# Attention scores in 32x32 tiles of TensorE, masks on three strips, masked blocks written once

## The reference, cut to what matters

```python
g = x @ Wg.T + bg;  v = x @ Wv.T + bv               # split in 16 heads of 8
corr = dot(g_i, g_j) / (|g_i| |g_j| + 1e-8)
m = (j <= i) & (j >= i - 128)                        # causal window of 128
corr = (corr * m + 1) / 2
denom = mean_j(corr) + 0.5
fitness_i = 1 / (denom_i * sum_i(1 / denom_i))
attn = softmax_j(corr_ij * fitness_i * m + (1 - m) * -1e10)
out = attn @ v
```

## Time and profile before

| | |
|---|---|
| median of 3 runs | 391.77 us (390.9 to 393.08) |
| profiled execution, its time | 388.9 us |
| its span, first to last instruction | 387.2 us |
| mean granted clock of TensorE | 0.933 |
| PE / DVE / ACT / POOL busy | 85% / 74% / 58% / 49% |
| matmuls | 2964 |

### The profile page before, as it was taken

The page is one execution under the profiler, slowest core; times in us unless marked ns, Lnnn a source line. Parts: engine busy times, 40 slices in busy tenths (PEclk is TensorE's granted clock), DMA queues, the critical chain, the costliest instruction groups (busy, mean ns, idle before and its releaser), DMA issues.

```text
span 387.2 us, 8903 instructions
## 1 busy us (share of the span) xinstructions
PE 329.0 (85%) x2964; PEld 195.8 (51%) x2964; DVE 285.7 (74%) x820; ACT 224.0 (58%) x498; POOL 188.0 (49%) x466
## 2 busy tenths in 40 slices
PE   6368786998899999999999999999998999857551
PEld 4233352554465656565656565656564656535341
DVE  1525547567879797979797979797979798889451
ACT  2034663466576767676767676767675777422210
POOL 7754033507273737373737474747473343543331
PEclk9999997799999999999999999999999999985555
DMA  4001000001000101010101010101010010000000
GB/s 117 27 1 29 14 2 3 27 2 29 1 30 3 42 1 42 2 44 1 42 2 43 1 43 2 43 0 30 3 29 13 15 30 2 14 14 3 14 14 17
DMA packets 12404, 7.62 MB, mean 20 GB/s; under 512 B 1026, under 2 KB 12356, under 8 KB 12356
## 3 DMA queue, kind: packets, MB, share of 16 engines
q1 hardware_dynamic: 12356, 7.03, 6.4%
HBM read 4.93 MB, written 2.10 MB: 18 GB/s over the span
## 4 chain that ended last, share of the span: by engine, by line
PE 34%; DVE 25%; POOL 18%; issue 13%; ACT 8%; POOLq 0%; ACTq 0%; DVEq 0%
PE OT L717 6%; PE S L694 5%; PE WA L824 4%; POOL nt L449 4%; PE S L698 3%; ACT Pm L545 3%; POOL rn L456 3%; POOL nt L451 3%; PE WC L737 2%; PE WD L795 2%; POOL nt L454 2%; POOL rstd L482 2%; DVE h L1065 2%; DVE xn L1113 2%; DVE A L1212 2%
## 5 line engine op out<-in xcount | busy, mean ns | idle before, releaser
L545 ACT ACTIVATE Pm<-S 128x384 f32<-128x384 f32 x256 | 111.8, 491 | 64.8 <-PE S L698 64.8
L694 PE MATMUL S<-mask,ident 128*128 128x384 f16 x256 | 65.8, 340 | 10.1 <-ACT Pm L545 7.9
L473 POOL TENSOR_TENSOR hq<-hm,hs 128x352 f32<-128x352 f32 x32 | 25.2, 787 | 66.0 <-DVE hm L1083 65.7
L717 PE MATMUL OT<-Pm,gv 128*32 128x256 f32 (+1 forms) x1024 | 56.8, 341 | 0.0
L698 PE MATMUL S<-BT,AT 32*128 32x256 f16 (+1 forms) x512 | 44.1, 251 | 0.0
L717 PEld LDWEIGHTS OT<-Pm,gv 128*32 128x32 f32 x1024 | 27.2, 111 | 21.2 <-issue 5.5
L698 PEld LDWEIGHTS S<-BT,AT 32*128 32x128 f16 x512 | 14.4, 93 | 42.9 <-issue 42.9
L694 PEld LDWEIGHTS S<-mask,ident 128*128 128x128 f16 x256 | 19.0, 99 | 33.7 <-issue 14.8
L1059 DVE SCALAR_TENSOR_TENSOR hh<-th,WC 128x352 f32<-128x352 f32 x32 | 16.6, 519 | 23.4 <-ACT th L563 23.3
L737 PE MATMUL WC<-wguT,xaT 128*128 128x352 f32 x64 | 29.1, 538 | 4.2 <-DVE h L1065 2.3
L795 PE MATMUL WD<-wdT,hqT 128*128 128x128 f32 (+1 forms) x192 | 29.6, 311 | 1.7 <-ACT hqT L593 1.7
(11 more groups left out here) (146 smaller groups left out, 715.0 us busy)
## 6 DMA issues: line engine op xcount, KB each, us to landing
xT<-x_turned_dram SPq DMA_DIRECT2D x16, 128.0 KB, 2.4
x_res<-x_dram SPq DMA_DIRECT2D x16, 128.0 KB, 2.1
out_dram<-yo SPq DMA_DIRECT2D x16, 128.0 KB, 2.1
wf<-w_down_dram SPq DMA_DIRECT2D x1, 176.0 KB, 2.5
wgv<-wgv_dram SPq DMA_DIRECT2D x1, 128.0 KB
wf<-w_gate_dram SPq DMA_DIRECT2D x1, 128.0 KB, 2.3
wf<-w_up_dram SPq DMA_DIRECT2D x1, 128.0 KB, 2.2
woT<-wo_dram SPq DMA_DIRECT2D x1, 64.0 KB
```

Of the source, the lines that this page charges most:

```text
L473: pool.tensor_tensor(b3(hq[:, k, 0:I]), b3(hm[:, k]), bc(hs[:, k], QB), ALU.mult).then_inc(s_hq, 1)
L545: act.activation(Pm[:, group % PR, hd % 4, :], S[:, (H * x + hd) % 3, 0:SCW], ACT.Exp, scale=1.0 / ZS).then_inc(s_exp, 1)
L694: pe.matmul(S[:, bank, 0:SCW], ident16[:, :], mask16[:, :], start=True, stop=False)
L717: i = pe.matmul(OT[VP * g:VP * (g + 1), T - (q1 - q0):T], gv_flat[:, at:at + VP], Pm[:, (GROUPS * x + c) % PR, g, q0:q1], start=(kt == 0 a ...
```

## The change

Three things change in `scores`, on PE:
- The dots come first, cut in groups of `KG = 32` keys. Each is a matmul on one 32x32 tile of the array (32 rows of the head, 32 keys): four tiles for keys 0 to 127 with the 160 queries that their window can reach, and four for keys 128 to 255 with 128, 96, 64 and 32 queries. So a pair has 16 of them.
- The mask comes last and only where a 32x32 block is partly masked: the diagonal blocks and the window's far edge, three strips of 32 columns in one matmul of 96 columns, one for each group of keys, eight for a pair. It uses the head's own row tile.
- Blocks that are wholly masked get no matmul. DVE writes them once, with nine memsets at the start (`s_far`), and nothing overwrites them. ACT waits for these before its first exp.

The semaphore `s_sc` is raised by the last mask matmul of a head. ACT's exp still reads all 384 columns.

```diff
+KG = 32
...
+        s_far = sem("s_far")
...
                 exps(t, 6)
                 if t == -1:
+                    act.wait_ge(s_far, 3 * (P // KG - 1))
                     exps(0, 0)
...
                 pair = [(2 * p + k, (H * x + 2 * p + k) % 3) for k in range(2)]
-                for hd, bank in pair:
-                    pe.matmul(S[:, bank, 0:SCW], ident16[:, :], mask16[:, :], start=True, stop=False)
-                for kt, (q0, q1) in enumerate(((0, T), (T, SCW))):
+                for kt in range(NT):
                     for hd, bank in pair:
                         r, c = 32 * (hd % 4), hd // 4
-                        i = pe.matmul(S[:, bank, q0:q1], AT[r:r + 32, x % 2, c, kt * P:(kt + 1) * P],
-                                      BT[r:r + 32, x % 2, c, T - (q1 - q0):T], start=False, stop=(kt == 1))
-                        if kt == 1:
-                            i.then_inc(s_sc, 1)
+                        for k0 in range(0, P, KG):
+                            at, n = (k0, P + KG) if kt == 0 else (T + k0, P - k0)
+                            q = kt * P + k0
+                            pe.matmul(S[k0:k0 + KG, bank, at:at + n], AT[r:r + 32, x % 2, c, q:q + KG],
+                                      BT[r:r + 32, x % 2, c, q:q + n], start=(kt == 0), stop=False)
+                near = mask16[:, :].rearrange("p (b c) -> p b c", c=P)
+                for n, (hd, bank) in enumerate(pair):
+                    m = 32 * (hd % 4)
+                    for k0 in range(0, P, KG):
+                        i = pe.matmul(S[k0:k0 + KG, bank, 0:SCW].rearrange("p (b c) -> p b c", c=P)[:, :, k0:k0 + KG],
+                                      ident16[m:m + KG, m:m + KG], near[m:m + KG, :, m:m + KG],
+                                      start=False, stop=True)
+                    i.then_inc(s_sc, 1)
...
         def _(dve):
+            for k0 in range(0, P, KG):
+                for a, b in ((0, k0), (k0 + P + KG, T), (T, T + k0)):
+                    if a < b:
+                        dve.memset(S[k0:k0 + KG, :, a:b], MASKED).then_inc(s_far, 1)
             dve.wait_ge(ld_b, 16 * 3)
```

## The result

The changed kernel takes 403.73 us (median of 4 runs, 401.97 to 404.55) against 392.38 for the kernel before on the same chip (390.9 to 393.08): ratio 1.0322, interval 1.0272 to 1.0372. It is slower by 11.4 us. The profiled execution took 401.97 us, its span is 400.3; before, 388.9 and 387.2.

A forecast was written before the change was run, and what follows sets the result against it. PE had almost no slack, but a chain through PE, ACT, DVE and POOL closed each turn. Terms: -4.0 - 1.6 - 2.5 + 11 - 0.15 + 2.0 = +4.75, 393.6 profiled, 396 median; range 390 to 402, overall 380 to 404.

The forecast's parts named there:

- A pair: PE's time for one pair of scores: 0.70 us before, 0.34 forecast, bounds 0.26 and 1.18.
- Rivals 2, 3 and 4: Pair costs 0.5 us: 386, chance 0.12; starts 25 ns apart: 392 to 393, 0.14; 49 ns: near 462, 0.05.
- The memsets: Nine DVE memsets of S at the start: some 3 us, all under the load of woT, cost 0.
- The clock in the loop: Main loop: PE's clock falls at the L818 wait, +1.1 us in 9 of 10 turns, +11; the eleventh -0.15.
- the chain's delay: PE work on the chain after L818, at low clock: between 0 and 3 us later, taken as 1.5.
- the saving in pair 6: The one pair of scores on the loop's chain gets shorter by 0.36 us a turn.
- The late stretch: 296 to 330 us, 16 pairs: PE could give 4.9 us, DVE's free time limits the gain to -2.5.
- the end: After 330 us, hanging on DVE and a slow PE: gain 0, an earlier clock fall +0.5 us.
- Falls in the first 62 us, where PE waits before many pairs, +1.5: Early part: clock falls at PE's waits before many pairs cost 1.5 us.
- the gains of 4.0 and 1.6: Shorter pairs on the chain: 12 in 24 to 62 us give -4.0, 5 in 67 to 84 us -1.6.
- Rival 1: The clock holds in spite of PE's waits: 379.2 us profiled, 382 as median; chance 0.27.
- The second circle: Loop through A, DVE's list, hh, seed, POOL, gh: 19.06 us a turn even with an infinitely fast scores step.

The follow-up runs named there:

- The experiment without masks: The kernel before with its mask matmuls left out, so its scores are unmasked: 400.88 us, ratio 1.0252.
- the two that give PE its work back: The changed kernel with fifteen unread matmuls ahead of PE's wait for xm: 390.08 us; the changed kernel with the old full-width masks issued as well: 390.88 us.
- the fills: Unread matmuls added to the changed kernel at the xm wait and in sequences 0 and 1: 385.6 us; with sixteen more before the weights' wait: 385.5 us.
- the kernel with wide dots: The changed kernel with strip masks kept but dots back in 32x128 tiles, far blocks unmasked: 404.7 us, ratio 1.0351.
- the profile with six fills: The changed kernel with six unread matmuls ahead of PE's wait for xm: nine executions at 390.5 to 394.1 us, two at 403.3 to 404.0, the profiled one among these.
- With the wait filled: The changed kernel with fifteen unread 256-column matmuls ahead of PE's wait for xm: 390.08 us, ratio 1.0008.
- the ramp filled: The changed kernel with four unread 256-column matmuls ahead of each pair's wait for ACT, sequences 0 and 1 only: 397.79 us, ratio 1.0244.
- both fills: The changed kernel with fifteen unread matmuls at PE's wait for xm and four ahead of each pair's wait in sequences 0 and 1: 385.6 us, ratio 0.9895.
- three: The kernel with both fills plus sixteen unread matmuls ahead of PE's wait for the gate and up weights: 385.5 us, ratio 0.9856.

## Why the prediction was right in direction and short in size

I had forecast +4.75 us; the profile has +13.1. As a median I had said 396, with 390 to 402 for this case; it is 403.73.

- **A pair.** Forecast 0.34 us, bounds 0.26 to 1.18; measured 0.28. Right, and a little too dear. Starts 3 to 4 ns apart held for eight matmuls on eight tiles; all 24 start within 0.149 us, which is 6.5 ns each, as reckoned. The Trainium skill's floor of about 25 ns ("TensorE: Matmul & The Clock Gate", "Wait — 56ns, not 53.3ns?") doesn't hold between different tiles; the 4 ns of the same page ("The mechanism") agree with the trace. Rivals 2, 3 and 4 fall with it.
- **The memsets.** Forecast some 3 us under the load of woT. DVE's first product starts at 4.67 us as before, and the memsets end at 3.15:

```profile
0.94 2.21 DVE L983 MEMSET S<- 32x288 f32 x9 [0.94 <-PEq L1521]
```

They took 2.21 us, all covered. Right.
- **The clock in the loop.** Forecast: a wait of 1.9 us at L818, the clock lost there in each turn, +1.1 a turn, +10.85 for the stretch. Measured 2.5 us, lost in each turn, 20.37 against 19.21, which is +1.16 in the turn shown, and +11.1 for the stretch. Right, in mechanism and size. Of its parts, the chain's delay was put at 1.5 and is 1.44 + 0.18 = 1.62 us; the saving in pair 6 was put at 0.36 and is 0.35. The experiment without masks and the two that give PE its work back show the cause. With the clock held a turn would be 18.8, so the low clock costs about 1.5 us a turn, of which the shorter pairs pay 0.4.
- **The late stretch.** Forecast -2.5, measured -1.8; the end, forecast +0.5, measured 0. Small misses.
- **The failed step** is "Falls in the first 62 us, where PE waits before many pairs, +1.5", beside the gains of 4.0 and 1.6: a net gain of 4.1 forecast up to 84 us, a loss of 3.9 measured. These 8.0 us are nearly the whole error of 8.3. The mechanism was named there and its size badly judged. Up to the fifth seed (63.85 us instead of 61.67) 2.2 us are lost where a net gain of 2.5 was forecast. Behind it another 1.7 are lost where 1.6 was to be gained: for that stretch the sum had no clock term at all, and the granted clock was 0.50 instead of 0.87 in 70 to 80. Up to 41 us the gain came, if less than reckoned: values start at 40.75 instead of 41.65, 0.9 against the 1.65 of five pairs at 0.33. Then the shorter pair leaves PE too little to do before ACT's exps are ready. The stretches of the changed kernel around it:

```profile
42.00:44.00 2.00, 0.69 (x27) 0.50 (x28) 0.64 (x2) 2.00 (x6) 0.00 (x0) 0.99 0.00 0
44.00:46.00 2.00, 1.94 (x41) 0.86 (x40) 1.86 (x6) 0.37 (x1) 0.96 (x4) 0.50 0.05 12
```

Before, PE was busy 1.36 us in 42 to 44 and stayed at 1.00 up to 62. Here it is busy 0.69, and half clock follows and lasts: 0.50 in 50 to 60 and again in 70 to 80. In the chain of waits from 24 to 62 us (start us, us, what) it looks so:

```profile
40.75 0.79 PE OT L727 x16
...
44.06 1.44 PE OT L727 x16
...
47.10 1.44 PE OT L727 x16
...
54.20 1.44 PE OT L727 x16
...
60.42 1.09 PE OT L727 x16
```

The five values of before that answer to these took 0.79 us each, so values alone give away 3 x 0.65 + 0.30 = 2.25 us. The other projections and turnings of PE on that chain, from these first values (40.75, before 41.65) on, add to 7.3 us instead of 4.1, another 3.1. The pairs on it did become cheaper, eight in 3.86 us where seven took 5.31, and that 1.5 is less than was lost. From the first values to the end of the last pair the chain takes 21.16 us instead of 17.75. All fourteen profiles say the same of this place. From the fourth to the fifth seed the seven with a clock of 1.00 in 40 to 60 us take 15.99 to 16.52 us, the seven with 0.60 to 0.66 take 19.35 to 20.26: the low clock costs about 3 us here. And with the clock held the short pairs (16.00 with four unread matmuls a pair, 16.52 before) win only 0.5. I had argued from the earlier trace rows that each of these pairs sits between waits, and had then taken the full gain of every pair in the same stretch, with 1.5 us set against it. The loop was worked out turn by turn; this stretch was not, though the same argument applies to it, and PE was emptier here (0.69 of 2 us) than in the stretch of the earlier trace rows that kept the clock (1.65 of 3 us).
- **Rival 1** (the clock holds, 382 us) is not what happened, but the fills show that its sum was roughly sound: with the clock held, 385.6 and 385.5 us measured. The rule of the Trainium skill that only gaps over about 3 us lose the clock ("TensorE: Matmul & The Clock Gate", "Why this matters for your kernels") would have given that case, and the trace contradicts it: waits of 2.5 us lost it in each turn, waits of 1.85 to 2.13 in six turns of the kernel with wide dots, and waits of at most 1.8 in the profile with six fills. The fills add work of their own and the early clock wasn't held throughout, so 382 itself was not tested.
- **The second circle**, of which PE is no part, I put at 19.06 us a turn. With the wait filled the turn is 18.80, and its chain of waits runs over DVE and POOL only: the circle was put 0.26 too long, and the saving in a turn is 0.4 instead of 0.15.

## What to carry to other kernels

Before work is taken off an engine whose clock follows its load, look where its new idle time will lie and what is issued right after it: where that work is on the chain, the shorter kernel can be the slower one, here by 10 us for leaving the masks out. Reckon a ramp turn by turn like the steady loop, and don't count a gain per step while a clock loss hangs over the same steps. Where nothing useful can be put into the wait without opening another, matmuls that nobody reads are worth a trial; here they turned a loss of 3.2% into a gain of 1.1%.

## What the runs showed that I had not expected

- Twenty-four matmuls on 32x32 tiles take 0.28 us with the way in and out; on different tiles most start 3 to 4 ns apart. Masks written in strips of 32 columns cost nothing that can be seen.
- How strongly the clock answers to little: waits of 1.8 us lost it, six matmuls of 256 columns in the wait left the time undecided from one execution to the next, fifteen held the clock nearly throughout (0.98). And the same wait of 2.52 us lost it in nine turns of one profile and kept it in one.
- The early stretch isn't the same in every execution. The kernels with the ramp filled, with both fills and with three have the same instructions up to the fifth seed, and their fourth seed came at 42.94, 45.94 and 46.19 us; the granted clock in 30 to 35 was 0.66 in the first, 1.00 in the two others. The first two differ again behind it: the sixth seed at 83.77 and 90.53, the clock 0.66 and 0.50 in 70 to 80. What decides it stays open, and a difference of up to 3 us in the early part of two single profiles is no evidence by itself.
